# Second list's exchanges two to a half step, its search in the last two steps, and another spread of the experts

## Chip, cores and metric

One core of one Trainium2 chip runs the whole program. The metric is the device time of one execution, in microseconds; the time of a kernel is the median of several executions.

## What is computed

The input is an image batch of 4 x 64 x 64 tokens with 128 channels. A layer norm and an involution-like convolution (weights made from the token itself, 3 x 3 taps, 16 groups) are added to it. On the resulting 16384 tokens a second layer norm feeds a graph attention that only routes, and a mixture of four experts:

```python
h = (x_flat @ W_gat).reshape(M, HEADS, NUM_EXPERTS)
src = concat([edge_index[0], loops]); dst = concat([edge_index[1], loops])   # 524288 edges + self loops
e = leaky_relu(a_src[src] + a_dst[dst], 0.2)
ee = exp(e - segment_max(e, dst)[dst]); denom = segment_sum(ee, dst)
agg = segment_sum(h[src] * (ee / denom[dst])[:, :, None], dst) + b_gat
scores = layernorm(agg).reshape(M, HEADS, NUM_EXPERTS).mean(1)
topk_s, topk_i = top_k(scores, 2); w = softmax(topk_s)
for ei in range(4):
    out += g[ei] * (gelu(x @ W1[ei] + b1[ei]) @ W2[ei] + b2[ei])       # 128 -> 256 -> 128
```

Each edge index is drawn from 0 to 32767, so half of the edges point to no token and are dropped.

## The kernel before

**Stages.** First the convolution with the node table (the image in 32 chunks of 512 tokens). Then each edge becomes one 32-bit key, its target above 14 bits of source, and the keys are cut into two lists of 262144: `short_runs` puts the smaller halves of short runs in the first list and the larger ones in the second. Nearly all edges that count are in the first list. Each list is sorted by target (a bitonic sort, 2048 keys on each of 128 partitions).

**The sort of a list** (`sort_runs`, `sort_levels`). VectorE does the compare passes (L1654, L1655, L1661). Between passes 14 exchanges carry the keys across partitions (`EXCHANGES`, numbered 0 to 13 for the first list, 14 to 27 for the second): TensorE transposes 16 blocks (L987), ScalarE copies them back (L1157, L1162, L1165), VectorE goes on. Behind an exchange of an even number VectorE has one to seven passes, one more at each further one; behind one of an odd number always eleven.

**Experts.** The 32 expert chunks run on TensorE (L998, L1005, L1008) and ScalarE (GELU L1180, copies L1188). They stand in the orders of these two engines after given exchanges, by the table `EXPERT_CHUNKS` (L81): its key -1 is ahead of all exchanges, 13 is behind the first list's last exchange (while VectorE runs `sort_runs(1)` and half step 0), and 15 to 27 are behind exchanges of the second list.

**Edge steps.** The sorted first list is worked through in steps of 16384 edges, each step k in two halves u = 0, 1. With these inputs there are 8 steps: `halves_of_steps` calls `half(k, u, j, pair, b)` with j = 0 to 3 for the first four steps, j = "loop" for steps 4 and 5 and j = -2, -1 for the last two, 6 and 7. I write a half step as (k, u). What each engine's `half` does, in this order:

- VectorE: its share of the second list's passes up to `SORTED_BY[(j, u)]`; a part of the second list's search, if one stands at this (j, u); for u = 0 `chain_runs(k - 1)` (L1957 to L1964 place the row to mend), for u = 1 and k > 1 `mend(k - 2)` (L1993 to L2003); then `edge_scans`: the dense products L1877 to L1884, a wait for the gathered rows (L1909), exponentials on ScalarE, L1938, L1946, and last `new_sources(k + 2, u)` (L1517 to L1533), which gives GpSimd the indices of the half step two steps on.
- GpSimd: `begin_half` (one gather of `adw`), 64 row gathers (`rows_of`, all at L768), then for u = 0 `fetch_fix(k - 2)`, which waits for `chain_runs(k - 2)`, or for u = 1 `store_fix(k - 2)`, which waits for `mend(k - 2)`; both from k = 2 on. Then the second list's search gathers, if they stand here (`find_rows(1, 2)`, `find_rows(1, 3)`, `windows`). The gathered rows have four buffers.
- ScalarE: its share of the exchanges with the experts behind them, then the exponentials of the half step. It runs `exchanges(0, 14)` with the experts of key 13 ahead of half step (0, 0).
- SyncE: loads for the step, then stores of the state, of the tails and flags of the runs, and `second_list`: `store_keys(1)` and the small round trips of the search.

**The second list's search** stands at four half steps, named by j: `BLOCKS_AT` (`find_blocks`; before it SyncE's `store_keys(1)` has stored the sorted keys and loaded samples), `RANK2_AT`, `RANK3_AT` (with `count_rounds`, `count_trips`), and `OWN_AT` (`find_nodes`, then `own_terms`, whose result SyncE stores to DRAM as `own_d` and loads back after the loop). After the loop the few edges of the second list are added one trip at a time (`trip`), the last two steps are mended, GpSimd gathers 128 columns of sums, and the outputs are mixed.

The lines that set the order are:

```python
SORTED_BY = {(0, 1): 4, (1, 0): 9, (1, 1): 14}
BLOCKS_AT, RANK2_AT, RANK3_AT, OWN_AT = (2, 0), (2, 1), (3, 0), (3, 1)
EXPERT_CHUNKS = {-1: 13, 13: 7, 15: 2, 17: 2, 19: 2, 21: 2, 23: 2, 25: 1, 27: 1}

if (j, u) != (0, 0):                                  # GpSimd's half
    begin_half(k, u, b)
    rows_of(2 * b + u)
...
if not isinstance(k, int) or k > 1:
    if u == 0: fetch_fix(k - 2, b)
    else:      store_fix(k - 2, b)
if (j, u) == BLOCKS_AT: find_rows(1, 2)
```

Of the kernel before, what the change touches and what calls it, by code (L numbers as in the profile page):

```python
# [33 lines left out]
P = 128  # L34
NB, NY, NX, C = 4, 64, 64, 128
M = NB * NY * NX
# [5 lines left out]
EDGES = ALL_EDGES // LISTS  # L42
# [16 lines left out]
T = 64  # L59
# [2 lines left out]
NEAR = 16  # L62
WORDS = NEAR * HEADS
PARTS = 2 + EXPERTS
SORTED_BY = {(0, 1): 4, (1, 0): 9, (1, 1): 14}
BLOCKS_AT, RANK2_AT, RANK3_AT, OWN_AT = (2, 0), (2, 1), (3, 0), (3, 1)
MAX_PAIRS = COLS // (4 * T)
ROUTES = 4
SCALED = 2
# [8 lines left out]
ROUNDS = -(-EDGES // WIN) + 1  # L78
KEYS_FROM = CHUNKS // 2 + 6
EXCHANGES = 2 * (LOG_E - LOG_C)  # L80
EXPERT_CHUNKS = {-1: 13, 13: 7, 15: 2, 17: 2, 19: 2, 21: 2, 23: 2, 25: 1, 27: 1}  # L81
SKIP = float(1 << 20)
TR, FA = True, False

# [1 line left out]
def some(n):  # L86

    return not isinstance(n, int) or n > 0


def metaformer_block(nc, x, Wr, br, gamma, beta, mean, var, Ws, bs, Wi, bi,
# [3 lines left out]
    with ctx:  # L95
        def sb(name, shape, dt=F32, where=ctx):
            return where.enter_context(nc.sbuf_tensor("sb_" + name, shape, dt))

        def dram(name, shape, dt=F32):
            return nc.dram_tensor("scr_" + name, shape, dt, kind="Internal").ap()  # L100
# [13 lines left out]
        own_d = dram("own", [M + P, NODE])  # L114
# [13 lines left out]
        node = sb("node", [P, TILES, NODE])  # L128
# [75 lines left out]
        trips_i = sb("trips_i", [1, 1], I32)  # L204
# [53 lines left out]
        state = sb("state", [P, 2, T, ST], F32, edge)  # L258
# [47 lines left out]
        def sems(names):  # L306
            return [sem(n) for n in names.split()]
# [31 lines left out]
        dch_in, dch_used, keys_in, state_out, tnT_back, y_out = (  # L339
            sems(f"{n}0 {n}1") for n in ("dch_in", "dch_used", "keys_in", "state_out", "tnT_back", "y_out"))  # L340
# [32 lines left out]
        state_steps = state_d.rearrange("(k p c) f -> k p c f", p=P, c=2 * T)  # L373
# [32 lines left out]
        def at_step(steps, k):  # L406

            return steps[ds(k, 1)].squeeze(0)
# [50 lines left out]
        def expert_chunks(n):  # L459

            first = sum(v for k, v in EXPERT_CHUNKS.items() if k < n)
            return first, first + EXPERT_CHUNKS.get(n, 0)

        assert sum(EXPERT_CHUNKS.values()) == PAIRS * CHUNKS

# [44 lines left out]
        def _(sp):  # L510
            def put(to, of, s):
                sp.dma_start(to, of).then_inc(s, 16)
# [77 lines left out]
            def store_keys(l):  # L590
                sp.wait_ge(keys_final, l + 1)
                sk = sorted_keys[l]
                with nc.allow_non_contiguous_dma(reason="one key per partition"):
                    put(level1_d[l].unsqueeze(1), sk[:, COLS - 1:COLS], levels_stored)
                put(level2_d[l], lvl2[:, l], levels_stored)
                put(keys_d[l][0:EDGES].rearrange("(p c) -> p c", p=P), sk, keys_stored)
                put(keys_d[l][EDGES:EDGES + COLS].unsqueeze(0), sk[P - 1:P, :], keys_stored)
                sp.wait_ge(levels_stored, 32 * (l + 1))
                sp.wait_ge(y_taken, ROWS * expert_chunks((1 + l) * EXCHANGES - 1)[1 if l else 0])
                put(samples, level1_d[l].partition_broadcast(P), samples_loaded)  # L600

            def load_keys(k, b):


                put(keyb[:, b, 1:], at_step(key_steps, k), keys_in[b])
                with nc.allow_non_contiguous_dma(reason="one key per run"):
                    if some(k):
                        put(keyb[:, b, 0:1], key_prev[ds(k * STEP_EDGES - 1, STEP_EDGES)].rearrange(
                            "(p c) -> p c", c=2 * T)[:, 0:1], keys_in[b])
                    else:  # L610
                        put(keyb[1:P, b, 0:1], key_prev[2 * T - 1:STEP_EDGES - 1].rearrange(
                            "(p c) -> p c", c=2 * T)[:, 0:1], keys_in[b])
# [24 lines left out]
            def half(k, u, j, pair, b):  # L637
                if u == 0:
                    for v in (0, 1):
                        if some(k):  # L640
                            sp.wait_ge(dch_used[v], k)
                        put(dch[:, v], at_step(starts_steps, k)[:, v * T:(v + 1) * T], dch_in[v])
                    if not isinstance(j, int) or j >= 0:
                        sp.wait_ge(sources_ready, 2 * k + 2)
                        load_keys(k + 2, b)
                    if some(k):
                        carries(k - 1, 1 - b)
                sp.wait_ge(state_ready, 2 * k + u + 1)
                put(at_step(state_steps, k)[:, u * T:(u + 1) * T], state[:, u], state_out[u])
                if u == 1:  # L650
                    with nc.allow_non_contiguous_dma(reason="one number per run"):
                        put(tails_d, state[:, 1, T - 1], tails_stored)
                        put(flags_d.unsqueeze(1), run_now[:, 2:3], tails_stored)
                        sp.wait_ge(tails_stored, 32 * (k + 1))
                        put(tails[:, :, :], tails_d.rearrange("p (h j) -> h p j", j=PARTS), tails_loaded)
                        put(whole[:, :], flags_d.partition_broadcast(HEADS), tails_loaded)
                second_list(j, u)

            def carries(k, b):
                sp.wait_ge(chain_ready, k + 1)  # L660
                put(chain_d.rearrange("p (h j) -> h p j", j=PARTS), chain[:, 0:P], chain_stored)
                sp.wait_ge(chain_stored, 16 * (k + 1))
                put(cprev[:, b], chain_d, cprev_loaded)

            def second_list(j, u):
                if (j, u) == (1, 1):
                    store_keys(1)
                with nc.allow_non_contiguous_dma(reason="one number per partition"):
                    if (j, u) == RANK2_AT:
                        sp.wait_ge(rank2_ready, 4)  # L670
                        put(widths_d, width[:, 2:4], widths_stored)
                        sp.wait_ge(widths_stored, 32)
                        put(widths[:, :, :], widths_d.unsqueeze(0), widths_in)
                        sp.wait_ge(block_ready, 4)
                        put(trips_d.unsqueeze(1), width[:, 0:1], widths_stored)
                        sp.wait_ge(widths_stored, 48)
                        sp.wait_ge(rounds_ready, 2)
                        put(widths[:, :, 0], trips_d.unsqueeze(0), widths_in)
                if (j, u) == OWN_AT:
                    sp.wait_ge(own_made, 1)  # L680
                    put(own_d[0:M].rearrange("(d j) f -> j d f", j=P), node[:, :, :], own_stored)
                    sp.wait_ge(trips_ready, 1)
                    trips = sp.value_load(trips_i[0:1, 0:1], min_val=1, max_val=EDGES)
                    put_back.append(trips)

            put_back = []

            tail = halves_of_steps(sp, lambda: sp.value_load(cnti[0:1, 1:2], min_val=FIRST_PAIRS, max_val=MAX_PAIRS - 2), half)
            sp.wait_ge(own_stored, 32)
            sp.wait_ge(trip_over, put_back[0])  # L690
# [208 lines left out]
        def _(pe):  # L899
# [115 lines left out]
            for n in range(EXCHANGES * LISTS):  # L1015
                exchange(n)
                if n == EXCHANGES - 1:
# [5 lines left out]
                    pe.wait_ge(search_over, 1)  # L1023
                elif n in EXPERT_CHUNKS:
                    pe.wait_ge(act_placed, 4 * (n + 1))
# [7 lines left out]
        def _(act):  # L1033
# [188 lines left out]
            def half(k, u, j, pair, b):  # L1222
                end = EXCHANGES + SORTED_BY.get((j, u), 0)
                if end > done[0]:
                    exchanges(done[0], end)
                    done[0] = end
                if (j, u) == OWN_AT:
                    act.wait_ge(own_scored, 1)
                    act.activation(hx[:, 0:2], hx[:, 0:2], ACT.Exp).then_inc(own_weighed, 1)
                if some(k):  # L1230
                    if u == 0:
                        chain_exponentials(k - 1)
                    elif not isinstance(k, int) or k > 1:
                        fix_exponentials(k - 2)
                edge_exponentials(k, u)
# [36 lines left out]
        def _(dve):  # L1272
# [736 lines left out]
            def half(k, u, j, pair, b):  # L2009
                end = SORTED_BY.get((j, u), 0)  # L2010
                if end > done[0]:
# [176 lines left out]
```

## Time and profile before

| | |
|---|---|
| median of 3 runs | 3184.3 us (3178.92 to 3187.57) |
| the profiled execution, its own time | 3176.01 us |
| its span, first to last instruction | 3174.2 us |
| VectorE busy | 2165.9 us (68%) |
| GpSimd busy | 1291.0 us (41%) |
| TensorE matmul busy | 998.8 us (31%) |
| ScalarE busy | 775.1 us (24%) |

The profiled execution is one run; its own time lies 8.3 us (0.26%) under the median. A view gives times in microseconds from the span's start. In a timeline row stand the start, the duration, the engine, the line, the operation, what it writes <- what it reads, and in brackets the engine's idle time ahead of it with what ended it. "issue" is idle time in which the engine waited for nothing that the profile shows.

### The profile page before, as it was taken

What the parts mean: (1) busy time and instruction counts of PE and PEld (TensorE: products, weight loads), DVE (VectorE), ACT (ScalarE), POOL (GpSimd) and SP (SyncE); (2) the same over time, 40 slices, a digit from 0 to 9 for tenths busy, and PEclk for the clock granted to TensorE, in tenths of its full rate; (3) what the DMA queues carried; (4) which work ended last, traced back from release to release, by engine and by line L of the source; (5) the groups of instructions that cost most, each with busy time, mean ns of one, the idle gap of its engine ahead of it and who ended that gap; (6) DMA issues with size and microseconds to landing.
All of it is one profiled execution on the core that took longest, in us unless ns stands there. A gap on an engine that the chain in (4) does not pass through costs nothing.

```text
span 3174.2 us, 21963 instructions
## 1 busy us (share of the span) xinstructions
PE 998.8 (31%) x4867; PEld 673.4 (21%) x4867; DVE 2165.9 (68%) x4009; ACT 775.1 (24%) x1568; POOL 1291.0 (41%) x1234
## 2 busy tenths in 40 slices
PE   6777784996111009465644100000000000000000
PEld 3444552664111006344423100000000000000000
DVE  6999889999999489978688563653243431421788
ACT  4555443443111004143322100000000000000344
POOL 0000000000000477777000077777777777763760
PEclk8777666998555559778967655555555555555555
DMA  2223239911000213223100212114121111104567
GB/s 65 70 76 77 68 106 390 150 69 63 0 0 0 22 25 79 58 52 58 65 31 30 45 18 24 26 17 32 18 22 18 22 18 22 18 7 101 146 207 233
DMA packets 259507, 202.36 MB, mean 64 GB/s; under 512 B 101592, under 2 KB 207445, under 8 KB 258902
## 3 DMA queue, kind: packets, MB, share of 16 engines
q1 hardware_dynamic: 189766, 114.21, 14.3%
q0 software_dynamic: 46336, 44.61, 8.9%
q10 hardware_dynamic: 23314, 42.60, 4.1%
q14 instruction: 67, 0.55, 0.1%
q8 instruction: 24, 0.39, 0.1%
HBM read 94.51 MB, written 107.07 MB: 64 GB/s over the span
## 4 chain that ended last, share of the span: by engine, by line
POOL 27%; DVE 25%; PE 16%; DVEq 12%; issue 11%; DMA 4%; ACT 3%; ACTq 1%; SPq 0%; POOLq 0%
POOL sb_rows_g L768 25%; PE bank L1008 5%; DVE sb_xi L1661 5%; DVE sb_xi L1654 5%; PE bank L998 5%; DVEq L1670 4%; DVE sb_inv L1359 2%; PE bank L924 2%; DVE sb_hid_y L1494 2%; DVEq L1390 1%; PE bank L987 1%; DVEq L1380 1%; DVE sb_y_new L2145 1%; DVE sb_stats L1332 1%; DVE sb_new L1882 1%
## 5 line engine op out<-in xcount | busy, mean ns | idle before, releaser
L768 POOL DMA_INDIRECT sb_rows_g<-scr_node,sb_srcs x1024 | 1085.6, 1060 | 312.1 <-issue 312.1
L1661 DVE TENSOR_TENSOR sb_xi<-sb_xi 128x512 f32<-128x512 f32 (+2 forms) x852 | 427.1, 568 | 67.1 <-ACT sb_xi L1157 53.4
L768 POOL DMA_INDIRECT sb_hid_y<-scr_level,sb_row_at x8 | 8.2, 1027 | 815.8 <-DVE sb_row_at L1418 813.9
L1909 DVE TENSOR_TENSOR sb_score<-sb_rows_g,sb_df 128x256 f32<-128x256 f32 x16 | 10.9, 681 | 470.7 <-DMA sb_rows_g<-scr_node,sb_srcs 470.4
L998 PE MATMUL bank<-sb_tnT_in,sb_w 128*128 128x512 f32 x512 | 239.6, 622 | 95.6 <-ACT sb_xi L1162 42.9
L1654 DVE TENSOR_TENSOR sb_xi<-sb_xi 128x1024 f32<-128x1024 f32 (+2 forms) x258 | 243.5, 944 | 28.1 <-ACT sb_xi L1162 11.3
L1008 PE MATMUL bank<-sb_w,sb_hid_y 128*128 128x128 f32 x2048 | 262.6, 282 | 0.0
L1008 PEld LDWEIGHTS bank<-sb_w,sb_hid_y 128*128 128x128 f32 x2048 | 238.3, 192 | 29.0 <-issue 29.0
L1655 DVE TENSOR_TENSOR sb_xi<-sb_xi 128x1024 f32<-128x1024 f32 (+2 forms) x258 | 243.9, 945 | 0.0
L1180 ACT ACTIVATE sb_hid_y<-bank,sb_b1c 128x512 f32<-128x512 f32 x256 | 164.1, 690 | 240.3 <-PE bank L998 238.4
L1203 ACT ACTIVATE sb_keep<-sb_drop 128x1280 f32<-128x1280 f32 x16 | 20.3, 1269 | 811.6 <-DVE sb_drop L1936 811.5
L987 PE MATMUL bank<-sb_ident,sb_xi 128*128 128x128 f32 x448 | 93.0, 390 | 364.4 <-DVE sb_xi L1655 207.9
L763 POOL DMA_DIRECT2D scr_adst_at_starts<-sb_zeros x1 | 1.1, 1057 | 474.3 <-DMA sb_xi<-in_L_ffn_edge_index 474.3
L1353 DVE TENSOR_TENSOR sb_prod<-sb_xi,sb_wv 128x1152 f32<-128x1152 f32 x128 | 172.7, 1349 | 17.3 <-ACT sb_xi L1063 12.6
L1359 DVE TENSOR_REDUCE sb_inv<-sb_prod 128x128 f32<-128x1152 f32 x128 | 172.0, 1344 | 5.9 <-issue 1.2
L987 PEld LDWEIGHTS bank<-sb_ident,sb_xi 128*128 128x128 f32 x448 | 80.0, 204 | 375.2 <-DVE sb_xi L1655 211.4
L768 POOL DMA_INDIRECT sb_agg<-scr_state,sb_posi x128 | 132.4, 1035 | 44.0 <-issue 38.7
L998 PEld LDWEIGHTS bank<-sb_tnT_in,sb_w 128*128 128x128 f32 x512 | 98.8, 200 | 215.7 <-issue 155.4
L924 PE MATMUL bank<-sb_wi,sb_xnT 128*128 128x128 f32 x768 | 136.5, 321 | 0.0
L1188 ACT ACTIVATE sb_y_new<-bank 128x512 f32<-128x512 f32 x128 | 76.4, 597 | 243.2 <-PE bank L1008 243.2
L1882 DVE TENSOR_TENSOR sb_new<-sb_keep,sb_adw 128x1024 f32<-128x1024 f32 x64 | 126.4, 1976 | 5.1 <-issue 0.4
L924 PEld LDWEIGHTS bank<-sb_wi,sb_xnT 128*128 128x128 f32 x768 | 110.0, 216 | 26.8 <-issue 26.8
(335 smaller groups left out, 1916.4 us busy)
## 6 DMA issues: line engine op xcount, KB each, us to landing
scr_expert_out<-sb_y_new ACTq DMA_DIRECT2D x64, 512.0 KB, 3.8
sb_y_in<-scr_expert_out SPq DMA_DIRECT2D x32, 1024.0 KB, 6.8
scr_state<-sb_zeros POOLq DMA_DIRECT2D x6, 4096.0 KB, 53.9
sb_rows_g<-scr_node,sb_srcs POOLq DMA_INDIRECT x1024, 2.4
scr_state<-sb_state SPq DMA_DIRECT2D x16, 768.0 KB, 3.3
scr_tnT<-sb_tnT SPq DMA_DIRECT2D x34, 256.0 KB, 2.0
sb_tnT_in<-scr_tnT ACTq DMA_DIRECT2D x34, 256.0 KB, 2.7
sb_xa<-in_x SPq DMA_DIRECT2D x64, 128.0 KB, 2.6
```

Source lines behind the costliest of these rows:

```text
L768: pool.indirect_dma_start(to, None, table, bass.IndirectOffsetOnAxis(ap=index, axis=0), **kw).then_inc(s, 16)
L924: last = pe.matmul(po[:, j * C:(j + 1) * C], xnT[:, u, r, 2 * j:2 * j + P], wi[:, :], start=FA, stop=j == 2)
L987: last = pe.transpose(bank[b][:, m * P:(m + 1) * P], src[:, (4 * b + m) * P:(4 * b + m + 1) * P], ident[:, :])
L998: pe.matmul(bank[n % 4][:, :], w1[:, e, a * P:(a + 1) * P], tnT_in[:, u], start=TR, stop=TR).then_inc(hid_psum, 1)
L1008: last = pe.matmul(po[:, e * C:(e + 1) * C], hid[u][:, 2 * e + a, r * P:(r + 1) * P], w2[:, e, a], start=FA, stop=e == EXPERTS - 1 and a == 1)
L1180: act.activation(hid[v][:, n], bank[n % 4][:, :], ACT.Gelu, bias=b1c[:, n // 2, n % 2:n % 2 + 1]).then_inc(hid_ready, 1)
L1353: return dve.tensor_tensor(to.rearrange("p (g f k) -> p g f k", g=GROUPS, k=KK), patch.rearrange("p (g f k) -> p g f k", g=GROUPS, k=KK), ...
L1359: dve.tensor_reduce(inv[:, r], prod[:, r % 2 * TAPS:(r % 2 + 1) * TAPS].rearrange("p (o k) -> p o k", k=KK), AX.X, ALU.add)
L1654: dve.tensor_tensor(vb[:, :, 0], va[:, :, 0], va[:, :, 1], ALU.min)
L1655: last = dve.tensor_tensor(vb[:, :, 1], va[:, :, 0], va[:, :, 1], ALU.max)
L1661: last = dve.tensor_tensor(vb[:, :, d, :, c], va[:, :, d, :, 0], va[:, :, d, :, 1], ALU.min if c == d else ALU.max)
L1882: dve.tensor_tensor(picked, hot, over(adw[:, w, h:WORDS:HEADS], T), ALU.mult)
```

## The change

`SORTED_BY` gives VectorE and ScalarE two exchanges of the second list in each half step from (0, 1) to (3, 1), where they had 4, 5 and 5 in (0, 1), (1, 0) and (1, 1). The four parts of the search move from steps 2 and 3 to steps 6 and 7 (j = -2, -1), on all engines. `store_keys(1)` moves from (1, 1) to (3, 1). One chunk of the experts more stands ahead of all exchanges, three more behind exchange 13, one in place of two behind 15, 17, 19, 21 and 23, and two in place of one behind 27. On SyncE the store of `own_d` and the read of the number of trips now come ahead of the wait for the state in their half step, and for u = 1 the state's second half is stored after the tails and flags.

```diff
-SORTED_BY = {(0, 1): 4, (1, 0): 9, (1, 1): 14}
-BLOCKS_AT, RANK2_AT, RANK3_AT, OWN_AT = (2, 0), (2, 1), (3, 0), (3, 1)
+SORTED_BY = {(0, 1): 2, (1, 0): 4, (1, 1): 6, (2, 0): 8, (2, 1): 10, (3, 0): 12, (3, 1): 14}
+BLOCKS_AT, RANK2_AT, RANK3_AT, OWN_AT = (-2, 0), (-2, 1), (-1, 0), (-1, 1)
...
-EXPERT_CHUNKS = {-1: 13, 13: 7, 15: 2, 17: 2, 19: 2, 21: 2, 23: 2, 25: 1, 27: 1}
+EXPERT_CHUNKS = {-1: 14, 13: 10, 15: 1, 17: 1, 19: 1, 21: 1, 23: 1, 25: 1, 27: 2}
...
+                if (j, u) == OWN_AT:
+                    sp.wait_ge(own_made, 1)
+                    put(own_d[0:M].rearrange("(d j) f -> j d f", j=P), node[:, :, :], own_stored)
+                    sp.wait_ge(trips_ready, 1)
+                    put_back.append(sp.value_load(trips_i[0:1, 0:1], min_val=1, max_val=EDGES))
                 sp.wait_ge(state_ready, 2 * k + u + 1)
-                put(at_step(state_steps, k)[:, u * T:(u + 1) * T], state[:, u], state_out[u])
-                if u == 1:
+                if u == 0:
+                    put(at_step(state_steps, k)[:, 0:T], state[:, 0], state_out[0])
+                else:
                     with nc.allow_non_contiguous_dma(reason="one number per run"):
                         put(tails_d, state[:, 1, T - 1], tails_stored)
                         put(flags_d.unsqueeze(1), run_now[:, 2:3], tails_stored)
+                        put(at_step(state_steps, k)[:, T:2 * T], state[:, 1], state_out[1])
...
             def second_list(j, u):
-                if (j, u) == (1, 1):
+                if (j, u) == (3, 1):
                     store_keys(1)
...
-                if (j, u) == OWN_AT:
-                    sp.wait_ge(own_made, 1)
-                    put(own_d[0:M].rearrange("(d j) f -> j d f", j=P), node[:, :, :], own_stored)
-                    sp.wait_ge(trips_ready, 1)
-                    trips = sp.value_load(trips_i[0:1, 0:1], min_val=1, max_val=EDGES)
-                    put_back.append(trips)
```

## Rows read from the trace of the kernel before

**Rows 1.** Page: shares of the chain, and GpSimd's two costliest kinds of gather.

```profile
POOL 27%; DVE 25%; PE 16%; DVEq 12%; issue 11%; DMA 4%; ACT 3%; ACTq 1%; SPq 0%; POOLq 0%
...
L768 POOL DMA_INDIRECT sb_rows_g<-scr_node,sb_srcs x1024 | 1085.6, 1060 | 312.1 <-issue 312.1
...
L768 POOL DMA_INDIRECT sb_hid_y<-scr_level,sb_row_at x8 | 8.2, 1027 | 815.8 <-DVE sb_row_at L1418 813.9
```

**Rows 2.** Who waited for whom, whole span: total us, times, longest us.

```profile
DVE sb_score L1909 <- DMA sb_rows_g<-scr_node,sb_srcs: 470.4, 11, 58.0
```

**Rows 3.** Timeline of GpSimd, from half step (2, 0) to the first trip.

```profile
1515.08 1.08 POOL L768 DMA_INDIRECT sb_rows_g<-scr_node,sb_srcs  x1 [0.30 <-issue]
1595.23 1.17 POOL L768 DMA_INDIRECT sb_fixs<-scr_state,sb_fix_i  x1 [79.07 <-DVE sb_fix_i L1964]
...
1827.06 0.96 POOL L768 DMA_INDIRECT sb_hid_y<-scr_level,sb_row_at  x1 [230.66 <-DVE sb_row_at L1418]
...
1932.17 0.95 POOL L768 DMA_INDIRECT sb_adw<-scr_adst,sb_first_i  x1 [0.30 <-issue]
...
2843.73 1.35 POOL L768 DMA_INDIRECT sb_trip_key<-scr_keys,sb_trip_i  x1 [0.30 <-issue]
```

**Rows 4.** Timeline of VectorE, second list's exchanges and the half steps between them.

```profile
1362.46 3.73 DVE L1661 TENSOR_TENSOR sb_xi<-sb_xi 128x128 f32<-128x128 f32 x11 [2.12 <-ACT sb_xi L1157]
...
1408.95 3.22 DVE L1661 TENSOR_TENSOR sb_xi<-sb_xi 128x128 f32<-128x128 f32 x13 [12.55 <-ACT sb_xi L1157]
...
1444.75 1.22 DVE L1877 TENSOR_TENSOR sb_keep<-sb_rel,sb_nearest 128x1024 f32<-128x1024 f32 x1
...
1478.22 1.87 DVE L1661 TENSOR_TENSOR sb_xi<-sb_xi 128x128 f32<-128x128 f32 x8 [2.25 <-ACT sb_xi L1157]
...
1527.21 2.84 DVE L1661 TENSOR_TENSOR sb_xi<-sb_xi 128x128 f32<-128x128 f32 x12 [10.53 <-ACT sb_xi L1157]
...
1578.78 14.93 DVE L1661 TENSOR_TENSOR sb_xi<-sb_xi 128x128 f32<-128x128 f32 x44 [11.02 <-ACT sb_xi L1157]
...
1632.01 0.69 DVE L1654 TENSOR_TENSOR sb_xi<-sb_xi 128x512 f32<-128x512 f32 x1 [2.63 <-ACT sb_xi L1162]
...
1671.98 2.24 DVE L1661 TENSOR_TENSOR sb_xi<-sb_xi 128x128 f32<-128x128 f32 x9 [12.54 <-ACT sb_xi L1157]
...
1764.56 0.19 DVE L1735 COPY sb_lvl<-sb_xi 128x32 f32<-128x32 f32 x1
```

**Rows 5.** Timeline around exchange 0: last expert chunk of key -1 on TensorE.

```profile
747.96 7.05 PE L998 MATMUL bank<-sb_tnT_in,sb_w 128*128 128x512 f32 x16
...
764.89 1.91 PE L987 MATMUL bank<-sb_ident,sb_xi 128*128 128x128 f32 x16
767.85 2.34 DVE L1661 TENSOR_TENSOR sb_xi<-sb_xi 128x128 f32<-128x128 f32 x7 [2.43 <-ACT sb_xi L1157]
```

**Rows 6.** Timeline: first expert matmuls of key 13, and ScalarE's first exponential behind them.

```profile
1183.43 2.93 PE L998 MATMUL bank<-sb_tnT_in,sb_w 128*128 128x512 f32 x3 [33.28 <-DVE sb_sinks L1766]
...
1350.35 1.28 ACT L1203 ACT_TABLE_LOAD   x1 [43.94 <-DVE sb_drop L1936]
```

**Rows 7.** Timeline of VectorE at (2, 1): from the first instruction of mend to edge_scans.

```profile
1864.22 0.16 DVE L1993 COPY sb_fixe<-sb_fixs 128x4 f32<-128x4 f32 x1
...
1865.70 1.23 DVE L1877 TENSOR_TENSOR sb_keep<-sb_rel,sb_nearest 128x1024 f32<-128x1024 f32 x1
```

**Rows 8.** Gathers of rows by group, in 1427:1516 (VectorE compares) and 2212:2299.

```profile
L768 POOL DMA_INDIRECT sb_rows_g<-scr_node,sb_srcs x64 | 70.0, 1093 | 19.5 <-issue 19.5
...
L768 POOL DMA_INDIRECT sb_rows_g<-scr_node,sb_srcs x64 | 67.6, 1056 | 19.5 <-issue 19.5
```

**Rows 9.** VectorE at (3, 1), where own_terms ends; own_d's store, us to landing.

```profile
2077.40 2.29 DVE L1811 TENSOR_TENSOR sb_node<-sb_hid_y 128x2048 f32<-128x2048 f32 x1
...
2119.37 0.68 DVE L1909 TENSOR_TENSOR sb_score<-sb_rows_g,sb_df 128x256 f32<-128x256 f32 x1 [20.52 <-DMA sb_rows_g<-scr_node,sb_srcs]
...
scr_own<-sb_node SPq DMA_DIRECT2D x1, 1536.0 KB, 17.4
```

## The prediction, made before the changed kernel ran

> **What bounds the kernel now.** I read the page first. The chain that ended last lies on GpSimd for 27% and on VectorE for 25% [rows 1]: no engine bounds the whole, they take turns. GpSimd's 1024 gathers of rows cost 1060 + 305 ns each, 1398 us in all, and its search gathers waited 814 us for VectorE [rows 1]. In the waits, VectorE waited 470 us in 11 places for gathered rows [rows 2]. So there is a stretch in which GpSimd waits for VectorE, and then one in which VectorE waits for GpSimd; the timeline of GpSimd shows the border [rows 3]. It ends the rows of (2, 0) at 1516.2, is idle 79.1 us for the row to mend that VectorE places in (1, 0), fetches it, and is idle another 230.7 us for `find_blocks(1)`, which stands behind all 14 exchanges. From 1827.1 to the first trip at 2843.7 it has eleven half steps of rows to gather and never waits again; VectorE waits for it in each of the eleven [rows 2]. Whatever lets GpSimd gather inside those 310 us comes off the end.
>
> On VectorE, 1360.3 (1362.46 less the wait of 2.12) to 1764.6 is the second list's exchanges with three half steps between them [rows 4]. Four of its starts were late by 10.5 to 12.6 us instead of the 2.1 to 2.6 seen where a half step lies between: the exchange stood on TensorE behind two expert chunks.
>
> **The change, step by step** (on the profiled execution's clock).
>
> *1. One expert chunk more ahead of exchange 0.* TensorE starts exchange 0 at 764.9, straight behind its 13th chunk, and VectorE, done 2.4 us before 767.9, waited only for the transposes and the copy [rows 5]: no slack. The last chunk took 764.89 - 747.96 = 16.9 us [rows 5]. I charge **17**; bounds 0 (hidden after all) and 19.
>
> *2. Three chunks more behind exchange 13.* Seven chunks took TensorE and ScalarE from 1183.4 to 1306.4 (1350.35 less 43.94 idle), 17.6 each [rows 6]. ScalarE must finish them before the exponentials of (0, 0), which it began at 1350.35 [rows 6]. Ten chunks end at 1306.4 + 3 x 17.3 = 1358.3. Cost **8** us; bounds 6 and 25 (a start above 1.5 of the marginal chunk). Exchange 14's transposes then follow at once and are ready before ScalarE gets to them.
>
> *3. VectorE up to the release of GpSimd.* GpSimd can now do the rows of (2, 1) straight after those of (2, 0): their indices come from (0, 1), and the search gathers no longer stand there. Behind them is `store_fix(0)`, which waits for `mend(0)` at VectorE's (2, 1), with ten exchanges ahead of it. From [rows 4]: exchanges 14+15 take 33.9 (to 1408.95 - 12.55), 16+17 35.8, 18+19 38.5, 20+21 40.6, 22 and 23 14.9 and 27.4; a half step with u = 1 takes 31.2 (1444.75 to 1475.97), one with u = 0 and its `chain_runs` 35.7 (1593.7 to 1629.4); mend takes 1.5 [rows 7]. One wait of 2.3 stands at each pair's start; the late starts of 10.5 to 12.6 go, since one chunk of 17 fits under eleven passes of 27. From 1360.3 + 25 = 1385.3:
> (0, 1) 2.3 + 33.9 + 31.2 = 67.4; (1, 0) 2.3 + 35.8 + 35.7 = 73.8; (1, 1) 2.3 + 38.5 + 31.2 = 72.0; (2, 0) 2.3 + 40.6 + 35.7 = 78.6; (2, 1) up to mend 2.3 + 42.3 + 1.5 = 46.1. Sum 337.9: **mend(0) is out at 1723.2**. GpSimd has ended (2, 1)'s rows at about 1625 and is idle 98 us, its last long wait.
>
> *4. GpSimd from there.* Its store takes 1.3, so (3, 0) begins at 1724.5. Before, from that same place at 1932.2 to the first trip at 2843.7 were 911.6 us [rows 3], with window gather, `find_nodes` and `own_terms` beside it. The change puts the eight `find_rows` gathers in: 8 x (1.03 + 0.3) = 10.6 [rows 1]. Gathers beside compare passes took 1093 ns, beside a quiet VectorE 1056 [rows 8]; (3, 0) and (3, 1) now run beside exchanges 24 to 27: 2 x 64 x 0.037 = 4.7. **Ready at 1724.5 + 911.6 + 10.6 + 4.7 = 2651.4.** The Trainium skill (SBUF — State Buffer, "Who interferes with whom") has a rule against this step: a VectorE instruction with two SBUF inputs and a GpSimd instruction that reads SBUF exclude each other, the later one blocked until the first ends. By it the gathers would stand behind the compares, and the sum would be that of rival C below; by the rows they lose 4.7.
>
> *5. Does GpSimd wait again?* (3, 1)'s store of the mended row needs VectorE's exchanges 24 to 27 (92.6 [rows 4]) and (3, 0): 1723 + 31 + 2.3 + 45 + 36 + 2.3 + 48 + 1.5 = 1889, and GpSimd gets there at 1724.5 + 2 x 91 = 1907 (911.6 / 10 a half step). No, by 18 us. Later each half step of VectorE has up to 58 us of slack [rows 2]. `store_keys(1)` has two steps of time, and the samples are there long before `find_blocks`.
>
> *6. The search in steps 6 and 7.* At (3, 1) `find_nodes` and `own_terms` stood ahead of `edge_scans`, and still VectorE waited 20.5 us for rows [rows 9]. At (7, 1) the order is the same: nothing on the path; if that cover went, 45 us of search would show. `own_d` is made at 2079.7, the rows were there at 2119.4, and its store needs 17.4 [rows 9]: it must be down before the trips. SyncE now issues it at once, so 39.7 against 17.4 hides it, with 22 us to spare; had SyncE kept it behind the state it would not. Tails ahead of the state shorten waits of `chain_runs` that lie under waits for rows: 0. The part behind the loop keeps its work: 0, bounds -5 and +10.
>
> **Sum:** 2651.4 - 2843.7 = -192.3. Check by idle time: 309.7 removed, 98 left, 17 moved by step 1: 309.7 - 98 - 17 = 195, less gathers slowed. Span 3174.2 - 192 = 2982, execution 2984. That execution lay 8.3 under the median of 3184.3, so the median should be 3184.3 - 192.3 = **2992 us**.
>
> **Rivals.**
> A. *The exchanges still start late*: experts or ScalarE hold five pairs by 10 us each up to (2, 1) [rows 4]. For: ScalarE's order has the experts ahead of the exponentials. Against: 17 us of experts under 27 of passes. 3042.
> B. *The tail shows*: the search at (7, 1) or the store of `own_d` outlasts the rows. For: slack only 20 to 22 us [rows 9]; a store twice as long, or a second round of windows (27 more), costs 10 to 45. Against: the same order hid at (3, 1). 3002 to 3037.
> C. *Gathers are locked out by compares*: 92.6 us of compares in (3, 0) and (3, 1) [rows 4] go to GpSimd in full. 2992 + 88 = 3080. It is the mechanism of the rule in step 4. Against: [rows 8].
> D. *Slower*: GpSimd loses its run-ahead. The place is its wait in `store_fix(k - 2)`; the price is that a half step's rows start only when VectorE enters that half step. Then from 1723: 31 for (2, 1); (3, 0) and (3, 1) take 47 or 50 plus 105 each (911.6 / 10 = 91 of rows, and behind them 14, an estimate: a little under half of the 31.2 of a half step); eight more half steps 105 each: 1723 + 31 + 307 + 840 = 2901, 57 later than now, 3241. It decides if a half step's rows wait for anything of the same half step. Against: VectorE waits up to 58 us for rows in every late half step [rows 2], so GpSimd is gathering for it while it stands there, and the indices come two steps early.
> E. *It does nothing that counts*: GpSimd's 310 us of idle time only move to another place, 3184. Against: step 5 finds no other wait.
>
> **Chances.** Forecast 0.80 (2960 to 3015 by the bounds of steps 1, 2, 4 and 6), A 0.06, B 0.07, C 0.02, D 0.03, E 0.02. The range takes in A and B: **2955 to 3045**. A change within 0.3% (10 us) can't be told from none here. Faster 0.95, same 0.02, slower 0.03.
>
> **What would show it.** Right: exchange 0 on TensorE near 782; the first exponential of key 13 near 1375; GpSimd idle once, some 98 us, ahead of the `store_fix` near 1723; then no GpSimd wait to the first trip at 2651; starts of pairs waiting 2 to 3 us; VectorE's last half step still waiting for rows. Wrong: a GpSimd wait behind (3, 1) or late in step 7, row gathers over 1.1 us in the mean, a trip key that waits for `own_d`, or a first trip later than 2700.

## The result, and the profile after

The changed kernel takes **2998.2 us** (median of 4, 2993.4 to 3007.6); the kernel before, in the same comparison, 3185.9 (3178.9 to 3191.3). The ratio is 0.942, with an interval of 0.939 to 0.945: 188 us less. The forecast was 2992, with 2955 to 3045.

The profiled execution is the slowest of the four, span 3005.8, and the profiled one of before was faster than every timed run. That matters when the clocks are laid side by side, so here are the two starts of the experts' work, which the change doesn't touch; first the kernel before, then the changed one, timeline of TensorE:

```profile
540.48 2.05 PE L998 MATMUL bank<-sb_tnT_in,sb_w 128*128 128x512 f32 x2 [18.19 <-DMA sb_tnT_in<-scr_tnT]
```

```profile
555.13 3.75 PE L999 MATMUL bank<-sb_tnT_in,sb_w 128*128 128x512 f32 x4 [17.63 <-DMA sb_tnT_in<-scr_tnT]
...
797.09 1.91 PE L988 MATMUL bank<-sb_ident,sb_xi 128*128 128x128 f32 x16
```

The first stage, with the same instructions, was 14.6 us longer in this execution. From there to exchange 0 it is 242.0 us, before 764.9 - 540.5 = 224.4 [rows 5]: **17.5 more** for one chunk, where 17 was said. (Behind SyncE's part of the file the lines are shifted by one: L768 is now L769, L1909 is L1910.)

The page of the changed kernel, beside [rows 1]:

```profile
L769 POOL DMA_INDIRECT sb_rows_g<-scr_node,sb_srcs x1024 | 1102.4, 1077 | 312.0 <-issue 312.0
...
L769 POOL DMA_INDIRECT sb_hid_y<-scr_level,sb_row_at x8 | 8.3, 1038 | 597.0 <-DVE sb_row_at L1419 594.8
```

GpSimd's wait for `find_blocks` in the edge steps is gone: 594.8 of the 597.0 is the one wait for the first list. A gather costs 17 ns more in the mean (1077 against 1060). VectorE's waits for rows, beside [rows 2], fell from 11 to 8:

```profile
DVE sb_score L1910 <- DMA sb_rows_g<-scr_node,sb_srcs: 338.8, 8, 63.1
```

GpSimd's timeline, beside [rows 3]:

```profile
1558.15 1.08 POOL L769 DMA_INDIRECT sb_fixs<-scr_state,sb_fix_i  x1 [0.30 <-issue]
...
1739.28 1.33 POOL L773 DMA_INDIRECT scr_state<-sb_fixo,sb_fix_i  x1 [86.27 <-DVE sb_fixo L2004]
1740.92 1.82 POOL L769 DMA_INDIRECT sb_adw<-scr_adst,sb_first_i  x1 [0.30 <-issue]
...
1928.72 1.02 POOL L773 DMA_INDIRECT scr_state<-sb_fixo,sb_fix_i  x1 [0.30 <-issue]
...
2671.24 1.02 POOL L773 DMA_INDIRECT scr_state<-sb_fixo,sb_fix_i  x1 [0.30 <-issue]
2672.57 1.27 POOL L769 DMA_INDIRECT sb_trip_key<-scr_keys,sb_trip_i  x1 [0.30 <-issue]
```

The mended row is fetched with no wait (before, 79.1 us), then comes the one wait of 86.3 us for `mend(0)`, and from 1739 to the first trip at 2673 none: 86 us of idle time where 310 were. The point to see is the name in the brackets, that of the instruction that ended the wait. Before, the long wait ended with L1418, a line of the second list's search; now it ends with `sb_fixo`, a line of `mend`.

VectorE's timeline: first the kernel before at the exponentials of (0, 0), then the changed kernel, beside [rows 4], [rows 6] and [rows 9]:

```profile
1353.25 2.29 DVE L1938 TENSOR_TENSOR sb_new<-sb_rows_g,sb_new 128x1024 f32<-128x1024 f32 x1 [2.98 <-ACT sb_new L1206]
```

```profile
1394.02 2.28 DVE L1939 TENSOR_TENSOR sb_new<-sb_rows_g,sb_new 128x1024 f32<-128x1024 f32 x1 [11.16 <-ACT sb_new L1207]
1403.22 2.05 DVE L1662 TENSOR_TENSOR sb_xi<-sb_xi 128x128 f32<-128x128 f32 x6 [2.11 <-ACT sb_xi L1158]
...
1470.26 1.87 DVE L1662 TENSOR_TENSOR sb_xi<-sb_xi 128x128 f32<-128x128 f32 x8 [2.28 <-ACT sb_xi L1158]
...
1694.05 2.23 DVE L1662 TENSOR_TENSOR sb_xi<-sb_xi 128x128 f32<-128x128 f32 x9 [2.11 <-ACT sb_xi L1158]
...
1738.22 0.18 DVE L2004 TENSOR_TENSOR sb_fixo<-sb_cprev,sb_fixs 128x20 f32<-128x20 f32 x1
...
1916.93 0.18 DVE L2002 TENSOR_TENSOR sb_cprev<-sb_cprev,sb_fixe 128x20 f32<-128x20 f32 x1 [13.05 <-ACT sb_fixe L1200]
...
2672.39 0.68 DVE L1910 TENSOR_TENSOR sb_score<-sb_rows_g,sb_df 128x256 f32<-128x256 f32 x1 [22.99 <-DMA sb_rows_g<-scr_node,sb_srcs]
```

Every pair of exchanges from (0, 1) to (3, 1) starts 1.8 to 2.3 us late and none by 10 or more (the rows show three of the seven). The wait for the exponentials of (0, 0) is 11.2 us, 8.2 more than the 3.0 it was before: the three chunks behind exchange 13. At (3, 1) `mend(1)` waits 13.05 us for ScalarE, which still has the two expert chunks behind exchange 27 ahead of it. In the last half step VectorE waits 23 us for rows, so the search is covered.

### The profile page after: what moved, and what is told of

It reads as the page before. It is cut to its first block, busy times and chain, and to the rows that moved or that the text cites. A ratio compares the mean times of both kernels' runs of the same rounds, so it can differ in the third digit from the quotient of the medians.

```text
span 3005.8 us, 22133 instructions
## 1 busy us (share of the span) xinstructions
PE 1023.6 (34%) x4867; PEld 690.9 (23%) x4867; DVE 2166.2 (72%) x4009; ACT 785.1 (26%) x1576; POOL 1310.5 (44%) x1234
## 4 chain that ended last, share of the span: by engine, by line
POOL 26%; DVE 23%; PE 19%; DVEq 11%; issue 11%; ACT 4%; DMA 4%; ACTq 1%; SPq 0%; POOLq 0%
POOL sb_rows_g L769 24%; PE bank L1009 6%; DVE sb_xi L1655 6%; PE bank L999 5%; DVEq L1671 4%; PE bank L925 2%; DVE sb_xi L1662 2%; DVE sb_hid_y L1495 2%; DVE sb_inv L1360 2%; DVEq L1391 1%; DVEq L1381 1%; PE bank L988 1%; PE bank L1006 1%; DVE sb_new L1883 1%; DVE sb_stats L1333 1%
## 5 line engine op out<-in xcount | busy, mean ns | idle before, releaser
L769 POOL DMA_INDIRECT sb_rows_g<-scr_node,sb_srcs x1024 | 1102.4, 1077 | 312.0 <-issue 312.0
L988 PE MATMUL bank<-sb_ident,sb_xi 128*128 128x128 f32 x448 | 99.7, 411 | 534.6 <-DVE sb_xi L1662 279.0
L769 POOL DMA_INDIRECT sb_hid_y<-scr_level,sb_row_at x8 | 8.3, 1038 | 597.0 <-DVE sb_row_at L1419 594.8
L1910 DVE TENSOR_TENSOR sb_score<-sb_rows_g,sb_df 128x256 f32<-128x256 f32 x16 | 10.9, 682 | 339.3 <-DMA sb_rows_g<-scr_node,sb_srcs 338.8
L769 POOL DMA_INDIRECT sb_agg<-scr_state,sb_posi x128 | 132.7, 1036 | 44.4 <-issue 38.7
L925 PE MATMUL bank<-sb_wi,sb_xnT 128*128 128x128 f32 x768 | 144.9, 335 | 0.0
```

Source lines behind the costliest of these rows:

```text
L769: pool.indirect_dma_start(to, None, table, bass.IndirectOffsetOnAxis(ap=index, axis=0), **kw).then_inc(s, 16)
L925: last = pe.matmul(po[:, j * C:(j + 1) * C], xnT[:, u, r, 2 * j:2 * j + P], wi[:, :], start=FA, stop=j == 2)
L988: last = pe.transpose(bank[b][:, m * P:(m + 1) * P], src[:, (4 * b + m) * P:(4 * b + m + 1) * P], ident[:, :])
```

## The experiments

The kernel before was timed again beside each of them; its median lay between 3177.1 and 3188.5. The changed kernel was not, so a difference of some 10 us from its 2998.2 is not shown by the medians alone. Where it matters I add a figure that leaves out both the first stage, which varied between 540.5 and 556.6 us in the twelve profiles of this study, and the end: the time from the experts' first matmul to the first trip in the profile. It was 2303.3 us in the kernel before and 2117.4 in the changed one. Single rows are compared counted from exchange 0.

**1. The search moved, the exchanges not spread.** With the old table of experts and SyncE's new order of stores. The cut is against the changed kernel:

```diff
-SORTED_BY = {(0, 1): 2, (1, 0): 4, (1, 1): 6, (2, 0): 8, (2, 1): 10, (3, 0): 12, (3, 1): 14}
+SORTED_BY = {(0, 1): 4, (1, 0): 9, (1, 1): 14}
...
-EXPERT_CHUNKS = {-1: 14, 13: 10, 15: 1, 17: 1, 19: 1, 21: 1, 23: 1, 25: 1, 27: 2}
+EXPERT_CHUNKS = {-1: 13, 13: 7, 15: 2, 17: 2, 19: 2, 21: 2, 23: 2, 25: 1, 27: 1}
...
-                if (j, u) == (3, 1):
+                if (j, u) == (1, 1):
                     store_keys(1)
```

> The kernel before with only the search moved to steps 6 and 7 and SyncE's new order; exchanges 4, 5, 5 and the old table of experts. My theory (GpSimd's release decides): GpSimd no longer stands at find_rows behind find_blocks in (2, 0), gathers the rows of (2, 1) early, and is released by mend(0) at VectorE's (2, 1). That comes at about 1796 + 36 + 1.5 = 1833 on the clock of the profile before; ten half steps follow, 911.6 + 10.6 + 1.3, first trip at 2757: 87 us less than before, 3097. GpSimd idle twice, 79 us in (1, 0) and some 220 us ahead of the store of mend(0). Rival (the search's place is worth only VectorE's wait of 28 us for the samples, the spread does the rest): 3156.

Measured 3131.6, ratio 0.982 (0.976 to 0.988): 55 us less, between the two theories. The wait was ended by the expected instruction; GpSimd's timeline of this run:

```profile
1866.70 1.33 POOL L773 DMA_INDIRECT scr_state<-sb_fixo,sb_fix_i  x1 [162.53 <-DVE sb_fixo L2004]
```

It came later than worked out. VectorE's timeline of this run at (2, 0) shows by what:

```profile
1826.71 0.16 DVE L1958 TENSOR_TENSOR sb_fix_f<-sb_run_now 128x1 f32<-128x1 f32 x1 [12.64 <-DMA scr_state<-sb_state]
...
1828.52 0.21 DVE L1967 TENSOR_SCALAR sb_whole<-sb_whole 4x128 f32<-4x128 f32 x1 [1.12 <-DMA sb_whole<-scr_flags]
```

`chain_runs` waits 13.8 us for the round trip of the last step's state and tails through DRAM. Before, that lay under VectorE's wait of 28.2 us for the samples in `find_blocks`; in the changed kernel a pair of exchanges stands between the state and `chain_runs` and covers it. My 36 us for (2, 0) had it at nothing. So the spread does more than shorten the way to `mend(0)`. How much it does in all can be read beside experiment 3, which has the same table of experts and differs from this one by the spread (and the place of `store_keys(1)`): 3131.6 against 3008.1, 123 of the 188 us. The spread with the search in its old place was not run. Exchange 0 lies 15.6 later here than in the profile before; with that taken off, `mend(0)` is at 1850 and the first trip at 2778, against 1833 and 2757. The other 11 us of the 32 missing are in how the medians lie to the profiles, and were not followed.

**2. The experts' table alone**, in the kernel before.

```diff
-EXPERT_CHUNKS = {-1: 13, 13: 7, 15: 2, 17: 2, 19: 2, 21: 2, 23: 2, 25: 1, 27: 1}
+EXPERT_CHUNKS = {-1: 14, 13: 10, 15: 1, 17: 1, 19: 1, 21: 1, 23: 1, 25: 1, 27: 2}
```

> The kernel before with only the new table of experts. My theory: exchange 0 is 17 us later and half step (0, 0) 8 us later, and the four late exchange starts (12.5 + 10.5 + 11.0 + 12.5 = 46.6 us) go to about 0, since one chunk fits under eleven passes: 46.6 - 25.5 = 21 us less, 3164. Rival (chunks moved ahead cost and give nothing back, since GpSimd bounds the rest): 3185 to 3211.

Measured 3157.6, ratio 0.990 (0.985 to 0.995): 29 us less. VectorE's long waits at the second list's exchange starts are gone here too: beside the 20.0 us at exchange 0, which now stands behind 14 chunks, 4.4 us in two waits are left of it. In the kernel before, where up to five exchanges follow one another, the table is worth something by itself, if no more than 1% (the interval leaves out 1).

**3. The changed kernel with the old table.**

```diff
-EXPERT_CHUNKS = {-1: 14, 13: 10, 15: 1, 17: 1, 19: 1, 21: 1, 23: 1, 25: 1, 27: 2}
+EXPERT_CHUNKS = {-1: 13, 13: 7, 15: 2, 17: 2, 19: 2, 21: 2, 23: 2, 25: 1, 27: 1}
```

> The changed kernel with the old table of experts (13, 7, 2, 2, 2, 2, 2, 1, 1). Two effects of opposite sign by my theory: exchange 0 17 us and half step (0, 0) 8 us earlier, but two chunks behind exchanges 17, 21 and 23 hold ScalarE until some 40 us after the exchange, while VectorE wants its exponentials of chain_runs or mend about 31 to 34 us after it: 6 + 6 + 13 us later. Net about 0: 2998, between 2990 and 3005. Rival 1 (two chunks hide under a pair and a half step): 2973. Rival 2 (the starts are late again by 10 us each, as in the kernel before): 3020 or more.

Measured 3008.1, ratio 0.945 (0.939 to 0.951): 10 more than the changed kernel, with intervals that overlap. From the first matmul to the first trip the two profiles agree (2117.6 and 2117.4 us), so in this order of the exchanges the new table is worth nothing that these runs show. What the old one saves ahead comes back as three waits for ScalarE, at `chain_runs` in (1, 0) and (2, 0) and at `mend(0)` in (2, 1), 31.6 us where I had said 25. VectorE's timeline of this run:

```profile
1487.75 0.81 DVE L1979 TENSOR_TENSOR sb_new<-sb_tails,sb_chain_e 4x640 f32<-4x640 f32 x1 [11.13 <-ACT sb_chain_e L1196]
...
1647.08 0.81 DVE L1979 TENSOR_TENSOR sb_new<-sb_tails,sb_chain_e 4x640 f32<-4x640 f32 x1 [9.18 <-ACT sb_chain_e L1196]
...
1736.65 0.18 DVE L2002 TENSOR_TENSOR sb_cprev<-sb_cprev,sb_fixe 128x20 f32<-128x20 f32 x1 [11.33 <-ACT sb_fixe L1200]
```

**4. SyncE's store of the state ahead of tails and flags again.**

```diff
-                if u == 0:
-                    put(at_step(state_steps, k)[:, 0:T], state[:, 0], state_out[0])
-                else:
+                put(at_step(state_steps, k)[:, u * T:(u + 1) * T], state[:, u], state_out[u])
+                if u == 1:
...
-                        put(at_step(state_steps, k)[:, T:2 * T], state[:, 1], state_out[1])
```

> The changed kernel with SyncE's order of the stores for u = 1 put back: the state ahead of the tails and flags. My theory: the waits of chain_runs for the state and the flags lie under VectorE's wait for rows, so 0: 2998 within 6 us. In the profile the long wait of chain_runs is again the one for the flags. Rival (chain_runs is on the path through the row that GpSimd fetches): 5 to 10 us more.

Measured 2995.3, ratio 0.940 (0.935 to 0.945): no difference. The waits changed places and lay under the wait for rows in either order; the first two rows are from the view of who waited for whom in the changed kernel, the next two from that of this one:

```profile
DVE sb_fix_f L1958 <- DMA scr_state<-sb_state: 37.5, 3, 13.3
...
DVE sb_whole L1967 <- DMA sb_whole<-scr_flags: 6.0, 3, 2.3
```

```profile
DVE sb_whole L1965 <- DMA sb_whole<-scr_flags: 30.3, 3, 10.2
DVE sb_fix_f L1956 <- DMA scr_state<-sb_state: 11.5, 3, 4.9
```

**5. Two chunks to where ScalarE has time.**

```diff
-EXPERT_CHUNKS = {-1: 14, 13: 10, 15: 1, 17: 1, 19: 1, 21: 1, 23: 1, 25: 1, 27: 2}
+EXPERT_CHUNKS = {-1: 13, 13: 9, 15: 2, 17: 1, 19: 2, 21: 1, 23: 1, 25: 1, 27: 2}
```

> The changed kernel with the experts' table 13, 9, 2, 1, 2, 1, 1, 1, 2 (keys -1, 13, 15, 17, 19, 21, 23, 25, 27): one chunk from ahead of exchange 0 goes behind 15, one from behind 13 goes behind 19. In (0, 1) and (1, 1) there is no chain_runs and no mend, and ScalarE is wanted only some 46 us behind the odd exchange, while two chunks end some 40 us behind it. My theory: 17 + 8 = 25 us less, 2973. Rival (any chunk behind an exchange costs what it costs ahead of it): 2998.

Measured 2969.5, ratio 0.933 (0.929 to 0.937): 29 us less than the changed kernel, and 28.5 in the profiles up to the first trip. Together with the third this tells the two costs apart: a chunk ahead of exchange 0 costs all of its 17 us, and a second chunk behind an odd exchange costs nothing in (0, 1) and (1, 1), but some 10 us where `chain_runs` or `mend` follows.

**6. mend ahead of the exchanges.** On VectorE and, with its exponentials, on ScalarE, in (2, 1) and (3, 1):

```diff
+                mended = u == 1 and end > done[0] and k > 1
+                if mended:
+                    mend(k - 2, b)
                 if end > done[0]:
                     sort_levels(1, done[0], end)
...
-                    elif not isinstance(k, int) or k > 1:
+                    elif not mended and (not isinstance(k, int) or k > 1):
                         mend(k - 2, b)
```

> The changed kernel with mend (and its exponentials on ScalarE) ahead of the exchanges instead of behind them in (2, 1) and (3, 1). My theory: only mend(0) holds GpSimd, so the release comes 44 us earlier (exchanges 22 and 23 and their start), and so does all behind it: 2955; GpSimd's wait ahead of that store falls from 86 to some 42 us, and mend(1) is out before GpSimd comes to it. Rival (VectorE's work as a whole bounds this stretch, the order in it does nothing): 2998.

Measured 2958.2, ratio 0.929 (0.925 to 0.933): 40 less. No work was taken out. In the profiles up to the first trip it is 45.5 less, and GpSimd's one wait fell from 86.3 to 44.3:

```profile
1693.87 1.07 POOL L773 DMA_INDIRECT scr_state<-sb_fixo,sb_fix_i  x1 [44.34 <-DVE sb_fixo L2007]
```

This is the plainest evidence that `mend(0)` set the end: only its place in two orders was changed.

**7. Exchange 23 behind the release**, moved from (2, 1) to (3, 0).

```diff
-SORTED_BY = {..., (2, 0): 8, (2, 1): 10, (3, 0): 12, (3, 1): 14}
+SORTED_BY = {..., (2, 0): 8, (2, 1): 9, (3, 0): 12, (3, 1): 14}
```

> The changed kernel with exchange 23 moved from (2, 1) to (3, 0). My theory: mend(0) is 27 us earlier, mend(1) is where it was (1917 in the profile), but GpSimd comes to it at 1902 instead of 1929, so it waits some 15 us there: 27 - 15 = 12 us less, 2986. A wait of GpSimd of 12 to 18 us at the store in (3, 1) must be seen. Rival 1 (slack enough): 2971. Rival 2 (the place of an exchange does nothing as long as their sum is the same): 2998.

Measured 2989.1, ratio 0.938 (0.934 to 0.942): 9 less, where 12 were expected. The interval overlaps that of the changed kernel (0.939 to 0.945); the profiles up to the first trip, 2108.2 against 2117.4, give 9 as well. GpSimd's timeline of this run has both waits:

```profile
1703.13 1.33 POOL L773 DMA_INDIRECT scr_state<-sb_fixo,sb_fix_i  x1 [61.72 <-DVE sb_fixo L2004]
...
1910.69 1.33 POOL L773 DMA_INDIRECT scr_state<-sb_fixo,sb_fix_i  x1 [21.51 <-DVE sb_fixo L2004]
```

The first is 24.6 shorter than in the changed kernel, the second is new, and over the 12 to 18 us expected. The slack at (3, 1) is a little smaller than was said.

**8. Five and six together**, to see whether the parts add up. It was run behind the ninth, and its text speaks of that one.

> The changed kernel with the moved experts (13, 9, 2, 1, 2, 1, 1, 1, 2) and mend ahead of the exchanges, but exchange 21 left in (2, 0): the last kernel but one without its third part. My theory: the parts add up, since both are work ahead of mend(0): 29 + 40 = 69 us less than the changed kernel, 2929, and GpSimd's wait ahead of the store of mend(0) is some 30 to 40 us; the third part was then worth 27. Rival (the parts overlap, the third did little): 2905.

Measured 2926.4, ratio 0.920 (0.914 to 0.927), GpSimd's wait 34.0 us. They add up: 69 expected, 72 by the medians, 67.7 by the profiles up to the first trip.

**9. And exchange 21 from (2, 0) to (2, 1)**, behind the mend that now stands first there.

```diff
-SORTED_BY = {..., (2, 0): 8, (2, 1): 10, (3, 0): 12, (3, 1): 14}
+SORTED_BY = {..., (2, 0): 7, (2, 1): 10, (3, 0): 12, (3, 1): 14}
```

> The changed kernel with the experts' table of the run before last (13, 9, 2, 1, 2, 1, 1, 1, 2), mend ahead of the exchanges in (2, 1) and (3, 1), and exchange 21 moved from (2, 0) to (2, 1). My theory: 25 + 44 + 27 = 96 us less, and GpSimd would then come to mend(1) about 4 us early and wait that: 2906, between 2900 and 2920. GpSimd's wait ahead of the store of mend(0) falls to about 15 us. Rival (with the wait at mend(0) nearly gone, the rows of (2, 1) or the mended row's fetch bound next, or VectorE in (4, 0)): 2930 or more.

Measured **2902.0**, ratio 0.913 (0.907 to 0.919): better than both kernels, 96 us under the changed one (92.9 by the profiles up to the first trip), 24 of them by this last move. GpSimd now waits almost nowhere between its first row and the first trip:

```profile
1627.69 1.24 POOL L773 DMA_INDIRECT scr_state<-sb_fixo,sb_fix_i  x1 [4.12 <-DVE sb_fixo L2007]
...
1817.51 1.02 POOL L773 DMA_INDIRECT scr_state<-sb_fixo,sb_fix_i  x1 [7.03 <-DVE sb_fixo L2007]
```

**10. own_d stored late.** The five lines of `OWN_AT` on SyncE put back behind the stores of the state and behind `second_list`:

```diff
-                if (j, u) == OWN_AT:
-                    sp.wait_ge(own_made, 1)
-                    put(own_d[0:M].rearrange("(d j) f -> j d f", j=P), node[:, :, :], own_stored)
...
                 sp.wait_ge(state_ready, 2 * k + u + 1)
...
                 second_list(j, u)
+                if (j, u) == OWN_AT:
+                    sp.wait_ge(own_made, 1)
+                    put(own_d[0:M].rearrange("(d j) f -> j d f", j=P), node[:, :, :], own_stored)
...
```

> The changed kernel with the store of own_d and the read of the number of trips back behind the state, tails and flags of (7, 1), as the kernel before had them in (3, 1). My theory: in the last half step nothing hides it any more. Before, it was issued 27.8 us after GpSimd's last row gather of its half step and landed 17.4 us later, so the first trip waits 45 us: 3043, and GpSimd shows a wait of some 45 us ahead of the first trip. Rival (the store's landing overlaps what follows the loop anyway): 2998 to 3010.

Measured 3022.5, ratio 0.950 (0.943 to 0.956): 24 more, about half of what was expected. The wait is there, in GpSimd's timeline of this run:

```profile
2711.45 0.96 POOL L769 DMA_INDIRECT sb_trip_key<-scr_keys,sb_trip_i  x1 [42.55 <-issue]
2716.86 0.94 POOL L769 DMA_INDIRECT sb_trip_rows<-scr_node,sb_trip_i  x1 [4.44 <-DVE sb_trip_i L1847]
```

42.6 us, but the trip behind it is shorter: VectorE had ended its last half step in the meantime, so the gather of the trip's rows waits 4.4 us for it, not 13.4, and the next step 4.1, not 12.8. Some 18 come back. I had priced the wait, not what it overlaps.

## Why the prediction was right

- **The bound and the release (steps 3 and 5).** Right. From VectorE's end of (0, 0) (1403.22 - 2.11) to `mend(0)` it took 337.3 us, where the sum said 337.9. Experiments 6 and 7 moved that one point by 44.6 and 28.4 us (counted from exchange 0), and the time went with it until the next wait. Rival E falls with them, and D with the profile: VectorE still waits for rows by up to 63 us.
- **Steps 1 and 2.** 17.5 for 17, and 8.2 for 8. (Step 2 counts its three chunks at 17.3 us, where the same rows give 17.6 each; that would have been 8.9.)
- **Late starts (rival A).** Not seen: 1.8 to 2.3 us at each pair. But the reason given, 17 of experts under 27 of passes, was half of it. Experiment 3 shows that two chunks don't make exchanges late in this order either; they make `chain_runs` and `mend` wait for their exponentials.
- **Step 4.** From the start of (3, 0) at 1740.9 to the first trip 931.6 us, where 926.9 were said: the term was short by 5. Most of that is its part for gathers beside compares. The rows of (3, 0) took 90.1 us from first to last, before 86.9; those of (3, 1) took 91.6, where the half step (4, 1), beside one `edge_scans` and nothing else, took 86.8. That is 8 us for 4.7. The reading of [rows 8] was wrong, too: its first stretch also holds the `edge_scans` of (0, 1), and by the trace of the kernel before the 19 gathers beside that took 1306 ns in the mean, the 45 beside compares 1003. That the price came out near is partly luck. Behind the first trip the kernel took 333.3 us, before 330.5.
- **Rival C.** Its price is refuted: 92.6 us were to be lost in (3, 0) and (3, 1), and 8 were. Its mechanism is not: gathers do stand behind compares, but seldom (last section).
- **GpSimd's idle time** was 86 where 98 were said. The rows of (1, 1), (2, 0) and (2, 1) took 91, 96 and 92 us instead of some 89 each, but ahead of a wait, where that cost nothing.
- **Slack at (3, 1)** was 11 us, not 18: step 5 forgot that ScalarE has two expert chunks behind exchange 27 and the mend's exponentials behind those, 13.05 us. GpSimd came some 6 us later than was said, which gave half of it back. That is also why experiment 7 waited 21.5 us there.
- **Step 6 and rival B.** Right: 23.0 us of VectorE's wait for rows is left in (7, 1), and `own_d`, stored at 2630.3, lands 16.0 later, 26 us ahead of the first trip. Experiment 10 shows that SyncE's new place for it is worth some 20 us.
- **The sum.** The errors above (0.5, 0.2, -0.6, 4.7 and 2.8) make 8 us; with the first stage's 14.6 they lead from the 2984 said for the profiled execution to 3006, and it took 3007.6. The median lay 6 above its forecast. How long the first stage was in the other three executions is not known.

## What to carry to other kernels

When one engine's in-order queue alternates between feeding another engine and waiting for it, find the one instruction that releases it and count only the work ahead of that. Work behind it is free until the next release; experiments 6 and 9 took some 40 and some 24 us without removing an instruction. Before filler work is put behind a step, look at what else its engine must do soon: two chunks kept ScalarE 35 to 37 us, which was free where its next exponential was wanted 49 us behind the last copy of the exchange (experiment 5, (0, 1) and (1, 1)) and cost 9 to 13 us where it was wanted 27 to 29 us behind it (experiment 3, and exchange 27 in the changed kernel). And work that is spread covers round trips that a block of it lays bare.

## What I had not expected of the hardware

**A gather that starts inside a VectorE instruction with two SBUF inputs waits for its end; compares mostly escape it by falling into step.** The groups of row gathers in three stretches of the changed kernel: (0, 1), beside the first list's index search, then compares of 128x512, 0.69 us each, and experts; then (2, 0), beside compares and more than one `edge_scans`; then (5, 0), beside one `edge_scans` and else little.

```profile
L769 POOL DMA_INDIRECT sb_rows_g<-scr_node,sb_srcs x64 | 62.5, 976 | 19.5 <-issue 19.5
...
L769 POOL DMA_INDIRECT sb_rows_g<-scr_node,sb_srcs x64 | 76.9, 1202 | 19.5 <-issue 19.5
...
L769 POOL DMA_INDIRECT sb_rows_g<-scr_node,sb_srcs x64 | 68.2, 1066 | 19.5 <-issue 19.5
```

The stretch without `edge_scans`, in which VectorE is hardly ever idle, has the fastest gathers, so the busy share of VectorE does not decide. The timeline of both engines, while GpSimd is in (5, 0) and VectorE ends (4, 1) and begins (5, 0), shows what does:

```profile
2120.09 2.83 DVE L1947 TENSOR_TENSOR_SCAN sb_sums_x<-sb_keep,sb_new 128x1280 f32<-128x1280 f32 x1
2120.72 2.95 POOL L769 DMA_INDIRECT sb_rows_g<-scr_node,sb_srcs  x1 [0.30 <-issue]
...
2147.74 1.97 DVE L1883 TENSOR_TENSOR sb_new<-sb_keep,sb_adw 128x1024 f32<-128x1024 f32 x1
2148.68 1.86 POOL L769 DMA_INDIRECT sb_rows_g<-scr_node,sb_srcs  x1 [0.31 <-issue]
2149.79 1.22 DVE L1885 TENSOR_REDUCE sb_drop<-sb_new 128x64 f32<-128x1024 f32 x1
2150.85 0.94 POOL L769 DMA_INDIRECT sb_rows_g<-scr_node,sb_srcs  x1 [0.30 <-issue]
2151.08 1.97 DVE L1883 TENSOR_TENSOR sb_new<-sb_keep,sb_adw 128x1024 f32<-128x1024 f32 x1
```

A gather takes 0.94 us. The one that started inside the scan ended 0.75 us behind it, the one that started inside a product ended 0.83 behind it, and so did all 56 gathers of this trace that started inside a product L1883 (0.82 to 0.84). The last gather above started just ahead of a product and took 0.94, though it ran beside it: what counts is which of the two started first. That agrees with the Trainium skill (SBUF — State Buffer, "Who interferes with whom"), by which an instruction with two SBUF inputs and a GpSimd instruction that reads SBUF exclude each other: the scan and the products have two SBUF inputs, and a gather reads its indices from SBUF. An index search `FIND_INDEX8`, whose row shows one input (128x1408), held none of the 60 gathers that started inside it (944 ns in the mean). No gather started early in a reduction, so no run here shows what that would do.

A compare has two SBUF inputs as well, and it does hold a gather. Both engines again, in (1, 0) of VectorE and the rows of (2, 0) of GpSimd:

```profile
1486.95 1.28 DVE L1656 TENSOR_TENSOR sb_xi<-sb_xi 128x1024 f32<-128x1024 f32 x1
1486.98 0.94 POOL L769 DMA_INDIRECT sb_rows_g<-scr_node,sb_srcs  x1 [0.30 <-issue]
1488.23 0.96 POOL L769 DMA_INDIRECT sb_rows_g<-scr_node,sb_srcs  x1 [0.30 <-issue]
1488.31 1.23 DVE L1655 TENSOR_TENSOR sb_xi<-sb_xi 128x1024 f32<-128x1024 f32 x1
1489.45 1.22 DVE L1656 TENSOR_TENSOR sb_xi<-sb_xi 128x1024 f32<-128x1024 f32 x1
1489.49 2.00 POOL L769 DMA_INDIRECT sb_rows_g<-scr_node,sb_srcs  x1 [0.30 <-issue]
```

The last one started 0.04 us into a compare, took 2.00 us and ended 0.82 behind it. But a gather starts every 1.25 us, and two compares together take 2.43, or 2.50 with gathers beside them: the two engines fall into step, and each gather then starts at the edge of a compare. Of the 130 gathers that started inside a 128x1024 compare in this trace 11 took over a microsecond, all ending 0.82 us behind it; the others started in its first 0.03 or its last 0.2 us. VectorE pays for it with some 0.06 us in a pair of compares.

**The first stage varies.** With the same instructions it ended (the experts' first matmul) between 540.5 and 556.6 us in the twelve profiles, while the first list's exchanges, from exchange 0 to the last compare, took 286.3 to 286.7 us in all of them. Most of the difference between the kernel before and the changed one arose at its very start: 13.0 of the 14.6 us were there by 80 us. From 22 to 41 us TensorE's matmuls of `sb_xnT` with `sb_wi` (L924, now L925) took 310 ns in the mean in the one and 450 in the other, while the granted clock shown for 20 to 40 us is close to full speed in both, 0.98 and 1.00. Why they were slower in one execution is open.
